# Second half of the causal heads by transfers instead of on-chip transposes, in a pass of a new order, and new order in the early stages

## The chip, the cores and the metric

The kernel runs on 1 core of a Trainium2 chip. The metric is the device time of one execution, in microseconds. A core has TensorE (PE in the profile), VectorE (DVE), ScalarE (ACT), GpSimd (POOL), SyncE (SP, which here issues nearly all DMAs) and 16 DMA engines. Each engine works through its own list of instructions in order; semaphores join them.

## The reference

Per batch (8 of them, 512 tokens x 256 features), all in float32:

```python
h = layernorm(x) * (1 + ca) + sa
x = x + ga * attention(h)          # 16 heads of 16, causal
h = layernorm(x) * (1 + cb) + sb
x = x + gb * ffn_block(h)
# ffn_block: xn = layernorm(h) * ln_g + ln_b
#   o = attention(xn) @ wo + h     # 32 heads of 8, not causal
#   y = gelu(o_half @ w1[e] + b1[e]) @ w2[e] + b2[e]   # two halves of a batch, expert e each
```

sa, ca, ga, sb, cb, gb are rows of silu(c) @ wmod, six per batch. Both attentions take an exact softmax: maximum, exponential, sum, division.

## The kernel before, in words

**Attention steps.** Work goes by *steps* `(b, a, s)`: batch b, a = 0 for the causal attention and 1 for the other, and s counting groups of 4 heads times 4 tiles of 128 queries or keys. A step has 4 slots, one per head. For each head the kernel runs `maxima` (scores by row, TensorE, and their maximum, VectorE), and 8 steps later `scores` (scores by column with the row maximum subtracted inside the matmul, TensorE, then exp on ScalarE), for the causal heads a mask on GpSimd, and `values` (probabilities times v, with a column of ones that gives the sums). Between maxima and scores the row maxima of a group of 4 steps go through DRAM: `max_rows` on GpSimd, `store_max` and, 4 slots later, `load_max` on SyncE, which writes them into q_stack. A group's first scores wait for that load. Full-width maxima take VectorE longer than causal ones, whose width is 128 to 512 keys.

**Normalised heads.** When a group's values are done, ScalarE copies bank_out to out_raw (`sums_out`). Then there are two ways. *By transfers*: out_raw is stored to DRAM (in `sums_out` on SyncE); when both groups of a chunk are there, `load_sums` brings the sums and the heads back with features on the partitions, `invert` (VectorE) takes the reciprocal, `store_inverse` and `load_inverse` spread it over the partitions through DRAM, and `scale_heads` (VectorE, L1806) multiplies. *On the chip*: `normalise` turns out_raw with four transposes (TensorE, L1529), VectorE takes the reciprocals (L1788) and multiplies (L1791), and `head_features` turns the result back with four more transposes (L1539), which ScalarE copies (L1314). `turned_on_chip` says which: before, for the causal heads, batch 0 and the second half (groups 2 and 3) of every batch go on the chip.

**Side work.** Everything else is put beside the steps at fixed slots: `qk` and `v` (projections), `to_features` (transposes of a normalised tile), `attention_out`, `ffn_sum`, `expert_in` with `gelu` (the "cluster"), `expert_out`, `layernorm` in 9 pieces, and the loads and stores. One unit of `qk`, `v`, `attention_out`, `ffn_sum` (a part) or `expert_out` (a part) is 4 matmul instructions. All but the cluster share one PSUM bank, bank_side. The Newton steps of a layernorm's square root run on GpSimd as one piece of 13 small operations, but for batch 0's second and third layernorm on VectorE, which also applies batch 0's modulation (`scale_and_modulate`).

**Stages.** After a prologue, `sections` lays out "before": the causal steps of batches 0, 1 and 2 (48 steps, from 73.5 us), then "run": a first pass of 32 steps of batch 0's second attention, passes n = 1 to 5 of 48 steps, and a tail. A pass has 16 steps of (n, 1), 8 of (n+2, 0), 16 of (n, 1), 8 of (n+2, 0); beside them go batch n+1's output, normalisations and projections, batch n-1's experts, and batch n+3's first normalisation and projections. In `place_pass` a number such as 93 means step 9, slot 3 of the pass. The placements are written out by hand; within half a step an engine meets first the scores, then the maxima, then values and the two hops of the maxima, then the side items.

Of the kernel before, what the change touches and what calls it, by code (L numbers as in the profile page):

```python
# [11 lines left out]
ALU = mybir.AluOpType  # L12
# [30 lines left out]
BATCHES = 8  # L43
SUM_COLUMNS = 64
# [11 lines left out]
NEWTON_PIECE = 3 + GUESS_STEPS  # L56
LN_PIECES = NEWTON_PIECE + 3

# [196 lines left out]
EARLY = 3  # L255
# [37 lines left out]
def place_pass(plan, first, n):  # L293
# [11 lines left out]
    place_units(plan, first, (71, 73), in_pieces("ffn_sum", e, 0))  # L305
    place_units(plan, first, (81, 83), in_pieces("ffn_sum", e, 1))
    place_units(plan, first, (172,), [("keep_x", n)])
    place_units(plan, first, (81, 83), layernorm_items(b, 1)[:2])
    place_cluster(plan, first, 93, e, 0, norm_under(b, 1))
    place_units(plan, first, (103, 111), [("ffn_input", b, 0), ("ffn_input", b, 1)])  # L310
    place_expert_out(plan, first, (101, 103, 113, 123), e, 0, 0)
    place_units(plan, first, (123, 131, 133, 133, 133, 133, 133, 153, 161), layernorm_items(b, 2))
    place_expert_out(plan, first, (133, 143, 153, 163), e, 0, 1)
    place_units(plan, first, (113, 183, 191), [("load_expert_in", e, 1), ("store_y", e, 0), ("load_expert_out", e, 1)])
# [3 lines left out]
    place_units(plan, first, (101, 131), [("load_residual", n + 2), ("load_mod", n + 2)])  # L318
# [19 lines left out]
def place_first_pass(plan):  # L338


    place(plan, 0, [("bias_part", 0, 0), ("load_expert_in", 0, 0), ("load_expert_out", 0, 0)], 0)
# [5 lines left out]
    place(plan, 18, [("load_x", 3)])  # L347
# [5 lines left out]
    place_at(plan, (45, 47), features_items(1, 1))  # L353
# [3 lines left out]
    place(plan, 77, [("stacks", 1, 2)])  # L357
    place_at(plan, (74, 91, 91, 105, 121), heads_items(0, 1, 0))
    place_at(plan, (87, 91, 95, 99), v_items(1, 1))
    place_norm(plan, (80, 82, 84, 85, 85, 85, 86, 94, 96), 3, 0)  # L360
    place(plan, 108, [("stacks", 1, 3)])
    place_at(plan, (101, 103), features_items(3, 0))
    place_at(plan, (105, 107, 109, 111, 115, 119, 123, 127), qk_items(0, 3))
    place(plan, 112, [("load_gate", 1)])
    place(plan, 130, [("keep_v", 1)])
    place_at(plan, (133, 141, 141, 147, 153), heads_items(0, 1, 1))
# [186 lines left out]
def build(nc, x, wq1, wk1, wv1, wo1, ln_g, ln_b, wq2, wk2, wv2, wo2, w1, b1, w2, b2, c, wmod, out):  # L553
# [28 lines left out]
    with ExitStack() as ctx:  # L582
# [193 lines left out]
        def previous_qk(a, b):  # L776


            if a == 0:
                return (1, b - 1) if b >= EARLY else (0, b)  # L780
# [1131 lines left out]
```

## Time and profile before

| | |
|---|---|
| median of 3 runs | 1524.27 us (1523.96 to 1528.13) |
| profiled execution | 1528.74 us, span 1526.7 us |
| TensorE clock granted, mean | 0.983 of full speed |
| DMA, whole run | 204.96 MB, mean 134 GB/s |
| stacks of a causal half batch | 4 DMAs of 256 KB (q) and 4 of 192 KB (k) |
| w_out | 1024 KB, 8.4 us from issue to landing |

The busy shares in 40 slices of the span (each digit is tenths, one slice is 38 us):

```profile
PE   6689798799999999999999999999999989998998
DVE  6577879898687887869687786878778697858621
PEclk9599899999999999999999999999999999999999
```

TensorE is filled less in the first eight slices than later, and its clock is lower in slices 1 and 4. From slice 10 (about 380 us) the picture repeats with each pass.

### The profile page before, as it was taken

The page shows a single profiled execution, that of the slowest core. Times are in us where ns is not written, and L with a number is a line of the kernel's source. Part 1 is how long each engine was busy: PE and PEld are TensorE (multiplying, and loading weights), DVE is VectorE, ACT ScalarE, POOL GpSimd, SP SyncE. Part 2 cuts the span into 40 slices and gives each one's busy share as a digit, 9 for nine tenths or more (in the row PEclk, how much of TensorE's full clock was granted, in tenths as well). Part 3 has the DMA queues.
Part 4 walks back from the last instruction along what each step waited for, and adds up shares of the span by engine and source line. Part 5 has one row for each costly group of instructions (what it writes and reads, how often), then busy time and mean ns, then how long its engine had stood idle before and what let it go on. Part 6 is the DMA issues. An engine that isn't in the chain of part 4 may idle for free.

```text
span 1526.7 us, 29704 instructions
## 1 busy us (share of the span) xinstructions
PE 1403.2 (92%) x9537; PEld 595.7 (39%) x9537; DVE 1143.9 (75%) x2889; ACT 994.3 (65%) x2074; POOL 485.3 (32%) x1217
## 2 busy tenths in 40 slices
PE   6689798799999999999999999999999989998998
PEld 5234242233434334343434334343344323342437
DVE  6577879898687887869687786878778697858621
ACT  1055466677667667776667666676767766767772
POOL 4145243334241334315332243413343133302100
PEclk9599899999999999999999999999999999999999
DMA  6856444347355453835645373654537242525230
GB/s 194 228 124 168 100 142 132 79 144 197 96 171 127 131 149 97 241 84 155 153 135 143 115 194 93 190 136 130 137 107 206 76 127 60 174 76 133 89 124 15
DMA packets 193886, 204.96 MB, mean 134 GB/s; under 512 B 58432, under 2 KB 143744, under 8 KB 193736
## 3 DMA queue, kind: packets, MB, share of 16 engines
q1 hardware_dynamic: 188072, 199.08, 47.8%
q10 hardware_dynamic: 5664, 3.98, 0.9%
q8 instruction: 82, 1.34, 0.4%
q14 instruction: 68, 0.56, 0.1%
HBM read 123.99 MB, written 79.02 MB: 133 GB/s over the span
## 4 chain that ended last, share of the span: by engine, by line
PE 71%; DVE 13%; ACT 7%; issue 3%; DMA 3%; SPq 2%; POOL 1%; DVEq 0%; ACTq 0%; POOLq 0%
PE bank_out L1519 17%; PE bank_scores L1497 13%; PE bank_max L1475 9%; PE bank_side L1436 8%; PE bank_side L1616 6%; DVE max_column L1760 5%; PE bank_max L1596 4%; PE bank_side L1449 3%; ACT probs L1294 3%; PE bank_side L1569 2%; PE bank_side L1596 2%; DVE bank_max L1757 2%; PE bank_side L1557 2%; PE bank_scores L1596 2%; PE bank_side L1411 1%
## 5 line engine op out<-in xcount | busy, mean ns | idle before, releaser
L1294 ACT ACTIVATE probs<-bank_scores 128x512 f32<-128x512 f32 (+3 forms) x1536 | 752.4, 543 | 286.1 <-PE bank_scores L1497 280.2
L1760 DVE TENSOR_REDUCE max_column<-bank_max 128x1 f32<-128x512 f32 x1024 | 653.1, 683 | 106.6 <-PE bank_max L1475 102.0
L1519 PE MATMUL bank_out<-probs,v_tile 128*9 128x512 f32 (+4 forms) x3072 | 364.8, 547 | 4.4 <-issue 1.7
L1475 PE MATMUL bank_max<-k_stack,q_stack 64*128 64x512 bf16 (+3 forms) x2048 | 313.0, 342 | 42.6 <-DVE max_column L1757 14.2
L1497 PE MATMUL bank_scores<-q_stack,k_stack 64*128 64x512 bf16 (+3 forms) x2048 | 315.0, 344 | 35.0 <-ACT probs L1294 34.3
L1757 DVE CUSTOM_DVE_ANT_0 bank_max<-bank_max,causal 128x384 f32<-128x384 f32 (+3 forms) x512 | 241.6, 514 | 103.0 <-PE bank_max L1475 100.9
L1497 PEld LDWEIGHTS bank_scores<-q_stack,k_stack 64*128 64x128 bf16 x2048 | 80.9, 93 | 417.5 <-issue 410.5
L1148 POOL CAST max_parts<-max_row 128x32 bf16<-128x32 f32 x96 | 23.0, 240 | 436.5 <-DVE max_row L1773 436.0
L1475 PEld LDWEIGHTS bank_max<-k_stack,q_stack 64*128 64x128 bf16 x2048 | 104.1, 95 | 116.9 <-issue 78.8
L1616 PE MATMUL bank_side<-w_out,hidden_T 128*128 128x256 f32 x448 | 126.6, 405 | 0.0
L1166 POOL TENSOR_SCALAR_AFFINE_SELECT probs<-probs 128x512 f32<-128x512 f32 x128 | 81.5, 637 | 58.6 <-ACT probs L1294 58.6
L1519 PEld LDWEIGHTS bank_out<-probs,v_tile 128*9 128x9 f32 (+1 forms) x3072 | 47.4, 91 | 129.4 <-issue 97.6
L1616 PEld LDWEIGHTS bank_side<-w_out,hidden_T 128*128 128x128 f32 x448 | 75.9, 189 | 44.6 <-issue 37.3
L1436 PE MATMUL bank_side<-act_T,wq 128*128 128x256 f32 x248 | 72.5, 416 | 8.3 <-DVE act_T L1729 3.7
L1436 PE MATMUL bank_side<-act_T,wk 128*128 128x256 f32 x244 | 70.4, 412 | 2.5 <-DVE rest L1743 1.0
L1757 DVE DVE_READ_ACCUMULATOR2_ANT max_column<- 128x1 f32 x512 | 72.1, 141 | 0.0
L1449 PE MATMUL bank_side<-wv,act_T 128*128 128x256 f32 x244 | 70.2, 411 | 0.5
L1256 ACT ACTIVATE partsq<-bank_side 128x256 bf16<-128x256 f32 x62 | 23.8, 385 | 68.2 <-PE bank_side L1436 68.0
L1134 POOL CAST partsq<-rest 128x256 bf16<-128x256 f32 x64 | 25.4, 396 | 119.0 <-DVE rest L1743 118.9
L1309 ACT ACTIVATE out_raw<-bank_out 128x512 f32<-128x512 f32 x96 | 57.9, 603 | 1.2 <-PE bank_out L1519 1.2
L1436 PEld LDWEIGHTS bank_side<-act_T,wq 128*128 128x128 f32 x248 | 43.8, 196 | 31.4 <-issue 10.5
L1596 PE MATMUL bank_max<-expert_xT,w_in 128*128 128x256 f32 x240 | 54.2, 379 | 0.0
(162 smaller groups left out, 1351.1 us busy)
## 6 DMA issues: line engine op xcount, KB each, us to landing
q_stack<-q_parts SPq DMA_DIRECT2D x124, 256.0 KB, 4.5
k_stack<-k_parts SPq DMA_DIRECT2D x124, 192.0 KB, 6.0
out_raw<-out_raw SPq DMA_DIRECT2D x74, 256.0 KB, 2.1
w_in<-in_L_ffn_w_dram SPq DMA_DIRECT2D x15, 1024.0 KB, 5.1
w_out<-in_L_ffn_w_dram SPq DMA_DIRECT2D x15, 1024.0 KB, 8.4
q_parts<-partsq SPq DMA_DIRECT2D x32, 384.0 KB, 2.7
k_parts<-partsk SPq DMA_DIRECT2D x32, 384.0 KB, 2.8
q_parts<-partsq SPq DMA_DIRECT2D x32, 256.0 KB, 3.1
```

Source lines behind the costliest of these rows:

```text
L1166: pool.affine_select(out=tile, in_=tile, compare_op=ALU.is_ge, fill=0.0, base=0, pattern=[[0, GROUP], [1, P]], channel_multiplier=-1).then ...
L1294: nc.scalar.activation(probs[s % 2][:, head_at(k), q0:S], region[bank][:, q0:S], ACT.Exp, scale=float(WIDTH[a]) ** -0.5).then_inc(drained[ ...
L1309: nc.scalar.activation(out_raw[:, g % 2, :], outb[:, :], ACT.Copy).then_inc(drained["out"], 1)
L1436: ins = pe.matmul(region[bank][:, 0:S // 2], w_qkv[a][t][:, cc, oc * P:(oc + 1) * P], act_T[:, cc, cols], start=(cc == 0), stop=(cc == C - 1))
L1449: ins = pe.matmul(region[bank][:, 0:D], act_T[:, cc, t * P:(t + 1) * P], w_qkv[a][2][:, cc, :], start=(cc == 0), stop=(cc == C - 1))
L1475: ins = pe.matmul(region[to][:, 0:keys], q_stack[buf][rows, at, qt * P:(qt + 1) * P], k_stack[buf][rows, at, 0:keys], start=(i == 0), stop ...
L1497: ins = pe.matmul(region[to][:, q0:S], k_stack[buf][rows, at, kt * P:(kt + 1) * P], q_stack[buf][rows, at, q0:S], start=(i == 0), stop=last)
L1519: ins = pe.matmul(outb[32 * k:32 * k + WIDTH[a] + 1, q0:S], v_tile[a][:, kt, g * GROUP + k, :], probs[s % 2][:, k, q0:S], start=(kt == 0), ...
L1596: ins = pe.matmul(region[bank][:, k * EXP_TOK:(k + 1) * EXP_TOK], w_in_of(b, j)[:, cc, ft * P:(ft + 1) * P], expert_xT[:, cc, j * EXP_TOK: ...
L1616: ins = pe.matmul(region[bank][:, 0:D], hidden_T[:, ft, k * P:(k + 1) * P], w_out_of(b, j)[:, ft, :], start=(ft == 0), stop=(ft == FT - 1))
L1757: v.tensor_tensor_reduce(region[bank][:, 0:keys], region[bank][:, 0:keys], causal[:, S - keys:S], 1.0, -3e38, ALU.add, ALU.max, dst).then_ ...
L1760: v.tensor_reduce(dst, region[bank], AX_X, ALU.max).then_inc(drained[bank], 1)
```

## The change

Four edits. (1) `turned_on_chip`: for batches 3 to 6 the second half of the causal heads goes by transfers; `attention_out` waits for both chunks. (2) `place_pass` in a new order: the transfer chain (b, 0, 1) at steps 2 to 8, `ffn_sum` before `attention_out`, the first cluster at step 12 instead of 9, and all that follows it later; features (b, 1) at steps 43 and 45. (3) Newton steps: never on VectorE; for the layernorms in NEWTON_APART GpSimd runs them in three parts with side slots of their own. Batch 0's modulation goes to GpSimd as for the other batches. (4) The early stages: slots moved; batch 3's first normalisation, features and q/k projections come earlier, its v comes into the first pass.

```diff
-        return b == 0 or g >= HEADS[0] // GROUP // 2
+        return b == 0 or g >= HEADS[0] // GROUP // 2 and not EARLY <= b < BATCHES - 1
+NEWTON_APART = ((2, 0), (0, 1), (0, 2), (3, 0), *((b, 2) for b in range(2, BATCHES - 1)))
...
 def place_pass
-    place_units(plan, first, (3, 13, 61, 63), v_items(0, n + 2))
-    place_units(plan, first, (13,), [("bias_part", n, 0)])
     if n > 1:
-        place_units(plan, first, (23,), [("head_features", b, 0, 1)])
-    place_units(plan, first, (33, 41, 43, 53), out_items(b))
+        place_units(plan, first, (3, 13, 63, 73), v_items(0, n + 2))
+        place_units(plan, first, (13,), [("bias_part", n, 0)])
+        place_units(plan, first, (21, 41, 41, 61, 81), heads_items(b, 0, 1))
+    place_units(plan, first, (83, 93, 103, 113) if n > 1 else (23, 33, 43, 53), out_items(b))
+    place_units(plan, first, (23, 33) if n > 1 else (83, 93), in_pieces("ffn_sum", e, 0))
+    place_units(plan, first, (43, 53) if n > 1 else (103, 113), in_pieces("ffn_sum", e, 1))
-    place_units(plan, first, (71, 73), in_pieces("ffn_sum", e, 0))
-    place_units(plan, first, (81, 83), in_pieces("ffn_sum", e, 1))
-    place_units(plan, first, (81, 83), layernorm_items(b, 1)[:2])
-    place_cluster(plan, first, 93, e, 0, norm_under(b, 1))
-    place_units(plan, first, (123, 131, 133, 133, 133, 133, 133, 153, 161), layernorm_items(b, 2))
+    place_units(plan, first, (111,), layernorm_items(b, 1)[:1])
+    place_cluster(plan, first, 123, e, 0, layernorm_items(b, 1)[1:])
+    place_units(plan, first, (151, 161, 161, 161, 161, 161, 161, 183, 191), layernorm_items(b, 2))
+    place_units(plan, first, (171, 173), [("newton", b, 2, 1), ("newton", b, 2, 2)])
-    place_units(plan, first, (171, 173), features_items(b, 2))
-    place_units(plan, first, (21, 93, 173, 251, 333, 423),
+    place_units(plan, first, (211, 221), features_items(b, 2))
+    place_units(plan, first, (23, 93, 173, 251, 333, 423),
                 [("stacks", n + 2, 0), ("stacks", n, 4), ("stacks", n, 5), ("stacks", n + 2, 1), ("stacks", n + 1, 2), ("stacks", n + 1, 3)])
-    place_units(plan, first, (181, 191, 201, 211, 221, 231, 241, 253), qk_items(1, b))
-    place_units(plan, first, (233, 251), features_items(b, 1))
-    place_units(plan, first, (263, 273, 283, 293), v_items(1, b))
+    place_units(plan, first, (231, 233, 241, 243, 253, 261, 263, 273), qk_items(1, b))
+    place_units(plan, first, (281, 283, 291, 293), v_items(1, b))
+    place_units(plan, first, (433, 453), features_items(b, 1))
...
 def place_first_pass
-    place_at(plan, (51, 53), features_items(1, 2))
-    place_at(plan, (55, 59, 63, 67, 71, 75, 79, 83), qk_items(1, 1))
+    place_at(plan, (59, 63), features_items(1, 2))
+    place_at(plan, (67, 71, 75, 79, 83, 87, 91, 95), qk_items(1, 1))
-    place_norm(plan, (80, 82, 84, 85, 85, 85, 86, 94, 96), 3, 0)
-    place_at(plan, (101, 103), features_items(3, 0))
-    place_at(plan, (105, 107, 109, 111, 115, 119, 123, 127), qk_items(0, 3))
+    place_at(plan, (1, 19, 23, 27, 31, 35, 39, 43), qk_items(0, 3))
+    place_at(plan, (47, 51, 53, 55), v_items(0, 3))
...
 def sections ("before")
-    place_norm(beside, (84, 88, 90, 91, 92, 93, 94, 98, 100), 0, 1)
-    place_norm(beside, (102, 104, 106, 107, 107, 107, 108, 114, 116), 0, 2)
-    place_at(beside, (117, 119), features_items(0, 2))
+    place_norm(beside, (82, 86, 87, 87, 87, 87, 87, 97, 101), 0, 1)
+    place_at(beside, (91, 95), [("newton", 0, 1, 1), ("newton", 0, 1, 2)])
+    place_at(beside, (99, 102, 103, 107), [("ffn_input", 0, t) for t in range(T_STEPS)])
+    place_norm(beside, (105, 110, 111, 111, 111, 111, 111, 121, 123), 0, 2)
+    place_at(beside, (115, 119), [("newton", 0, 2, 1), ("newton", 0, 2, 2)])
+    place_at(beside, (125, 129), features_items(0, 2))
+    place_norm(beside, (138, 142, 143, 143, 143, 143, 143, 155, 159), 3, 0)
+    place_at(beside, (147, 151), [("newton", 3, 0, 1), ("newton", 3, 0, 2)])
+    place_at(beside, (185, 189), features_items(3, 0))
...
 GpSimd
-                if piece == NEWTON_PIECE and not (b == 0 and n):
-                    for step in range(GUESS_STEPS, ROOT_STEPS):
+                if piece == NEWTON_PIECE:
+                    last = GUESS_STEPS + 5 if (b, n) in NEWTON_APART else ROOT_STEPS
+                    for step in range(GUESS_STEPS, last):
                         newton_step(pool, b, n, step)
+            def newton(b, f, n, turn):
+                for step in range(GUESS_STEPS + 1 + 4 * turn, GUESS_STEPS + 5 + 4 * turn):
+                    newton_step(pool, b, n, step)
...
 TensorE, attention_out
-                if (b, 0, 0) in scaled_number:
-                    wait(pe, heads_made, scaled_number[b, 0, 0] + 1)
+                for cc in range(C):
+                    if t == 0 and (b, 0, cc) in scaled_number:
+                        wait(pe, heads_made, scaled_number[b, 0, cc] + 1)
...
 VectorE: scale_and_modulate and the Newton steps of batch 0 are taken out
```

## Rows read from the trace of the kernel before

**Rows 1.** The page: busy time by engine; the chain that ended last.

```profile
PE 1403.2 (92%) x9537; PEld 595.7 (39%) x9537; DVE 1143.9 (75%) x2889; ACT 994.3 (65%) x2074; POOL 485.3 (32%) x1217
...
PE 71%; DVE 13%; ACT 7%; issue 3%; DMA 3%; SPq 2%; POOL 1%; DVEq 0%; ACTq 0%; POOLq 0%
```

**Rows 2.** Stretches: length; busy PE, PEld, DVE, ACT, POOL; clock, DMA share, GB/s.

```profile
140.00:190.00 50.00, 41.37 (x350) 17.81 (x352) 39.39 (x170) 23.66 (x61) 14.74 (x30) 0.90 0.55 120
...
192.00:242.00 50.00, 46.72 (x418) 20.05 (x419) 40.87 (x117) 32.08 (x83) 21.34 (x47) 1.00 0.46 128
...
243.00:286.00 43.00, 33.77 (x230) 10.16 (x230) 38.81 (x86) 28.38 (x55) 21.06 (x56) 1.00 0.47 126
...
292.00:298.00 6.00, 6.00 (x32) 2.04 (x30) 2.58 (x4) 3.78 (x7) 0.00 (x0) 0.72 0.16 49
...
573.68:750.28 176.60, 170.54 (x1181) 71.36 (x1180) 139.33 (x353) 124.33 (x259) 61.48 (x155) 1.00 0.52 143
```

**Rows 3.** TensorE's timeline: start, length, line, operation, count, [idle before].

```profile
266.33 1.05 PE L1519 MATMUL bank_out<-probs,v_tile 128*9 128x512 f32 x8
...
269.11 1.05 PE L1519 MATMUL bank_out<-probs,v_tile 128*9 128x512 f32 x8
...
291.78 0.63 PE L1411 MATMUL bank_side<-ident,normed 128*128 128x128 f32 x4 [3.12 <-DVE normed L1707]
...
345.68 1.13 PE L1436 MATMUL bank_side<-act_T,wk 128*128 128x256 f32 x4 [0.40 <-DVE rest L1743]
...
1325.73 1.05 PE L1519 MATMUL bank_out<-probs,v_tile 128*9 128x512 f32 x8
...
1328.85 1.05 PE L1519 MATMUL bank_out<-probs,v_tile 128*9 128x512 f32 x8
...
1334.79 0.61 PE L1475 MATMUL bank_max<-k_stack,q_stack 64*128 64x512 bf16 x2 [2.17 <-DMA k_stack<-k_parts]
...
1335.33 1.89 PE L1519 MATMUL bank_out<-probs,v_tile 128*9 128x512 f32 x8
```

**Rows 4.** Groups by line in 140 to 190 us, VectorE.

```profile
L886 DVE TENSOR_SCALAR root<-root 128x4 f32<-128x4 f32 x6 | 1.0, 170 | 0.2
...
L1672 DVE SCALAR_TENSOR_TENSOR normed<-normed,rstd,mod_bc 128x256 f32<-128x256 f32 x4 | 2.1, 568 | 0.0
```

**Rows 5.** Groups by line, whole run.

```profile
L1729 DVE TENSOR_SCALAR act_T<-bank_side,mod_cur 128x512 f32<-128x512 f32 x15 | 12.1, 807 | 2.5 <-PE bank_side L1411 2.0
...
L1529 PE MATMUL bank_max<-ident,out_raw 128*128 128x128 f32 x88 | 14.4, 286 | 0.7 <-ACT out_raw L1309 0.7
```

**Rows 6.** TensorE's waits in one pass (573.68 to 750.28): total, times, longest.

```profile
PE bank_side L1436 <- ACT act_T L1281: 0.5, 1, 0.5
...
PE bank_side L1539 <- DVE x_in L1791: 0.4, 1, 0.4
```

**Rows 7.** SyncE's timeline of DMA issues, start of pass 3.

```profile
722.84 2.58 SPq L860 DMA_DIRECT2D q_stack<-q_parts  x4
...
727.52 0.43 SPq L963 DMA_DIRECT2D w_out<-in_L_ffn_w_dram  x1
...
730.85 3.71 SPq L1061 DMA_DIRECT2D max_rows<-max_parts  x3
...
739.30 0.58 SPq L1071 DMA_DIRECT2D q_stack<-max_rows  x2
```

**Rows 8.** A 3 us stretch inside those issues.

```profile
727.00:730.00 3.00, 3.00 (x19) 1.12 (x18) 2.62 (x6) 1.57 (x3) 0.97 (x3) 1.00 1.06 229
```

**Rows 9.** Timeline: a load_max, the scores that waited for it, and step 8's scores.

```profile
102.50 0.57 SPq L1071 DMA_DIRECT2D q_stack<-max_rows  x2
...
104.35 0.61 PE L1497 MATMUL bank_scores<-q_stack,k_stack 64*128 64x512 bf16 x4 [0.17 <-DMA q_stack<-max_rows]
...
743.26 0.39 PE L1497 MATMUL bank_scores<-q_stack,k_stack 64*128 64x512 bf16 x2
```

More of the change, by code:

```diff
@@ L43 @@
 BATCHES = 8
+EARLY = 3
 SUM_COLUMNS = 64
@@ L448, in sections @@
     place_at(beside, (1, 5, 9), qk_items(0, 1)[5:])
-    place_at(beside, (15, 19, 27, 31), v_items(0, 1))
+    place_at(beside, (13, 17, 21, 29), v_items(0, 1))
     place(beside, 3, [("load_x", 2)])
-    place(beside, 12, [("stacks", 1, 0)])
-    place(beside, 43, [("stacks", 1, 1)])
+    place(beside, 18, [("stacks", 1, 0)])
+    place(beside, 39, [("stacks", 1, 1)])
     place(beside, 40, [("load_gate", 0)])
-    place_norm(beside, (14, 18, 22, 24, 24, 25, 26, 32, 34), 2, 0)
-    place_at(beside, (41, 43), features_items(2, 0))
@@ L456, in sections @@
-    place_at(beside, (45, 49, 53, 57, 61, 65, 69, 71), qk_items(0, 2))
+    place_norm(beside, (14, 18, 19, 19, 19, 19, 19, 29, 31), 2, 0)
+    place_at(beside, (23, 27), [("newton", 2, 0, 1), ("newton", 2, 0, 2)])
+    place_at(beside, (33, 37), features_items(2, 0))
+    place_at(beside, (41, 45, 49, 53, 57, 61, 65, 69), qk_items(0, 2))
     place(beside, 67, [("first_v", 1)])
     place_at(beside, (73, 75), [("head_features", 0, 0, 0), ("head_features", 0, 0, 1)])
-    place(beside, 76, [("stacks", 2, 0)])
@@ L460, in sections @@
-    place_at(beside, (77, 79, 81, 83), out_items(0))
-    place_norm(beside, (84, 88, 90, 91, 92, 93, 94, 98, 100), 0, 1)
-    place_at(beside, (85, 89, 93, 97), v_items(0, 2))
-    place_norm(beside, (102, 104, 106, 107, 107, 107, 108, 114, 116), 0, 2)
+    place(beside, 72, [("stacks", 2, 0)])
+    place_at(beside, (77, 79, 81, 85), out_items(0))
+    place_norm(beside, (82, 86, 87, 87, 87, 87, 87, 97, 101), 0, 1)
+    place_at(beside, (91, 95), [("newton", 0, 1, 1), ("newton", 0, 1, 2)])
+    place_at(beside, (99, 102, 103, 107), [("ffn_input", 0, t) for t in range(T_STEPS)])
@@ L464, in sections @@
+    place_at(beside, (89, 97, 105, 113), v_items(0, 2))
+    place_norm(beside, (105, 110, 111, 111, 111, 111, 111, 121, 123), 0, 2)
+    place_at(beside, (115, 119), [("newton", 0, 2, 1), ("newton", 0, 2, 2)])
     place_at(beside, (104, 118, 118, 128, 140), heads_items(1, 0, 0))
-    place(beside, 107, [("stacks", 2, 1)])
+    place(beside, 102, [("stacks", 2, 1)])
     place(beside, 110, [("load_residual", 1)])
-    place_at(beside, (117, 119), features_items(0, 2))
-    place_at(beside, (121, 125, 129, 133, 137, 141, 145, 149), qk_items(1, 0))
+    place_at(beside, (125, 129), features_items(0, 2))
@@ L469, in sections @@
+    place_at(beside, (131, 133, 137, 141, 145, 149, 153, 157), qk_items(1, 0))
     place(beside, 130, [("load_mod", 1)])
     place(beside, 131, [("first_v", 2)])
-    place(beside, 138, [("stacks", 0, 2)])
+    place(beside, 146, [("stacks", 0, 2)])
     place(beside, 143, [("head_features", 1, 0, 1)])
-    place_at(beside, (153, 157, 161, 165), v_items(1, 0))
+    place_at(beside, (161, 165, 169, 173), v_items(1, 0))
     place(beside, 170, [("stacks", 0, 3)])
-    place_at(beside, (169, 173), features_items(0, 1))
+    place_at(beside, (177, 181), features_items(0, 1))
@@ L1169, in ffn_input @@
             def ffn_input(b, f, half):
-                for t in range(2 * half, 2 * half + 2):
-                    wait(pool, normed_made[1], T * (b - 1) + t + 1)
+                tiles = range(half, half + 1) if b == 0 else range(2 * half, 2 * half + 2)
+                for t in tiles:
+                    wait(pool, normed_made[1], T * b + t + 1)
                     pool.tensor_tensor(ffn_x[:, t, :], normed[1][:, t, :], mod_bc[:, 1, :], ALU.mult).then_inc(ffn_scaled, 1)
-                for t in range(2 * half, 2 * half + 2):
+                for t in tiles:
                     wait(pool, ffn_scaled, T * b + t + 1)
@@ L1663, in first_guess @@
                 ins.then_inc(rstd_made[n], 1)
-            def scale_and_modulate(half):
-                for t in range(2 * half, 2 * half + 2):
-                    v.scalar_tensor_tensor(out=ffn_x[:, t, :], in0=x1[:, t, :], scalar=mean_var[:, 1, t, 0:1],
-                                           in1=mod_bc[:, 1, :], op0=ALU.subtract, op1=ALU.mult).then_inc(ffn_scaled, 1)
-                for t in range(2 * half, 2 * half + 2):
-                    wait(dve, ffn_scaled, t + 1)
-                    v.scalar_tensor_tensor(out=ffn_x[:, t, :], in0=ffn_x[:, t, :], scalar=rstd[:, 1, t:t + 1],
-                                           in1=mod_bc[:, 2, :], op0=ALU.mult, op1=ALU.add).then_inc(ffn_x_made, 1)
             def layernorm(b, f, n, piece):
@@ L1694, in layernorm @@
                 elif piece == NEWTON_PIECE:
-                    if b == 0 and n:
-                        for step in range(GUESS_STEPS, ROOT_STEPS):
-                            newton_step(dve, b, n, step)
+                    pass
                 else:
@@ L1702, in layernorm @@
                     dst = normed[n % 2]
-                    if n == 1 and b == 0:
-                        scale_and_modulate(half)
-                        return
                     for t in range(2 * half, 2 * half + 2):
```

36 lines of the change are left out of this document (18 added, 18 removed).

## The prediction

> **What bounds the kernel now.** I read the page first (busy time by engine, chain of waits), then the busy time in chosen stretches, then the waits of TensorE inside one pass, then the timeline of SyncE's transfers. TensorE is busy for 1403.2 of 1526.7 us and carries 71% of the chain [rows 1], but that share is an average of two regimes. In a pass (48 steps; four of them repeat to within 0.02 us) TensorE is busy 170.54 of 176.60 us, VectorE 139.3 and the DMA engines 52% [rows 2]: there, only TensorE's work and its few waits count. In the early stages it is different: in 140 to 190 us TensorE is idle for 8.6 us and its clock is 0.90; in 243 to 286 it is idle for 9.2 us while VectorE is busy for 38.8 of 43 [rows 2]. A step of the non-causal heads takes 3.12 us with one side unit of work (1328.85 less 1325.73) and still 2.78 with none (269.11 less 266.33) [rows 3], since VectorE's maxima fill it. TensorE's own work in a bare step is about 3.12 - 1.06 = 2.06, so a bare step wastes 0.7 us, and where side work stands counts as much as how much there is.
>
> **The early stage (to about 242 us).** (a) Batch 0's two normalisations lose their Newton steps on VectorE: 26 small operations, each 0.17 us with a gap to 0.2, so 5.2 us [rows 4]. (b) scale_and_modulate goes: 8 operations of 0.56 become 4 of about 0.41 (a pass over the same tile), so 2.9 us less. Together VectorE is relieved of 8.1 us, in the stretch 140 to 190 in which TensorE idles 8.6 us and loses a further 5.0 us to the clock (0.10 of 50) [rows 2, 4]. GpSimd takes the Newton steps in three parts and 8 multiplies and adds of a tile; it works 14.7 of 50 us there before [rows 2], so has the time, and its causal masks, queued behind them, have about a step of slack before the values need them. v and output units are also spread one to a step. Bounds: 0 if the masks come late, -13.6 if all is recovered; I take -8.5, near VectorE's relief. (c) Steps 0 to 18 are filled a little more evenly: -1.5 (0 to -3). (d) Batch 3's first normalisation and its two feature transposes come in from the first pass: on VectorE 8 statistics and scalings of 0.41, aggregates and guesses, 4.4 us, and two act_T copies of 0.8 [rows 5]; on TensorE two sets of transposes of 0.6. 192 to 242 has 9.1 us of VectorE free and 3.3 of TensorE [rows 2]. Between +1.2 and +6.0; I take +3. Sum -7.
>
> **The first pass (32 steps, 243 to 360 us).** Its steps 0 and 4 to 10 have no side unit; q and k of batch 3 now stand there, and only steps 30 and 31 stay bare. (d)'s 6.0 us of VectorE are gone, the features of batch 1 no longer wait for a fresh normalisation: that wait was 3.12 us, and the clock behind it 0.72 for 6 us, 1.7 us more [rows 2, 3]. Lost now: 9.2 + 3.1 + 1.7 and some 3 us elsewhere, 17 us. Against this, four v units of 1.06 come in from pass 1 and 1.2 us of transposes leave, +3. If 11 of 17 are recovered: -8 (-3 to -12).
>
> **Pass 1.** Less: four v units 4.2, two sets of normalise transposes 1.2. But steps 0, 1, 6, 7 are now bare: +4 x 0.7 = 2.9. With the edits common to all passes (below, without the transfer chain): -1.5 (-4 to +1). The loads of batch 3's stacks are as tight here, at most +1.
>
> **Passes 2 to 5, each.** Removed: 2 normalise sets and 1 head_features set. A set is four 128x128 transposes; 22 sets took 14.4 us, 0.65 each, 0.6 without the overlap with their neighbours [rows 5]: -1.8. ScalarE's copy of the heads goes; VectorE gets invert and scale_heads for two reciprocals and two products: nothing, as the one has 52 us free in a pass and the other 37. Waits that go with them: x_in 0.4; act_T 0.5, since the features now stand a step ahead of q and k [rows 6]; -0.9, and some 0.5 of smaller ones. Added: q and k now stand in twos within steps 23, 24 and 26. Two such units in a step cost a wait of 0.40 for the bank, as in the row [rows 3]: +1.2. Batch b's second normalisation moves from steps with causal maxima to steps 16 to 19, whose maxima are full width: VectorE has 14.5 us of work there against 12.5 of steps; +0.8 (0 to 2). Two steps hold only features: +0.3. Without the transfer chain's waits each pass gives -0.4 to -0.9; I take -0.9.
>
> Now the transfers. In steps 2 to 5 SyncE issues, in this order: the stacks of batch n+2 at 722.84, w_out at 727.52, store_max at 730.85, load_max at 739.30 [rows 7]. Stacks and w_out are 1.8 and 1.0 MB; the DMA engines are full (share 1.06, 229 GB/s) [rows 8], so store_max takes 3.71 to issue and load_max waits until 739.30. Its rows are usable 1.85 us after its issue starts (102.50 to 104.35), so at 741.15, and step 8's scores, which need them, start at 743.26 [rows 9]: 2.1 us of slack. After the change two side units (6 to 8 were in twos) and two sets of transposes are gone from these eight steps, so step 8 comes 2 x 1.05 + 2 x 0.6 + 0.4 = 3.7 us earlier: 739.6. The transfers are no sooner: the out_raw store, sums and heads loads of batch n+1 are put ahead of the stacks (0.29 MB more in the burst, 1.2 us at that rate, and the load waits for its store to land, 0.7 to 1.7). With nothing added the stall is 1.6; with all of it 4.4. I take 2.9: TensorE waits in every pass for max_rows at step 8. Behind it scale_heads waits for inverse_T, issued after that same load_max; it lands within the stall, so I give it nothing (up to 1). After such a wait the clock may fall: behind the 2.17 us wait at 1334.79 the 1.05 us of values took 1.89 [rows 3], about 2.5 us in all; +1.3 between 0 and 2.5.
>
> The Trainium skill, "DMA: Bandwidth & Descriptors", Queues, rings and completion order, says that each DMA engine consumes its descriptors in ring order. By that rule the 8 KB of max_rows queue behind the 2.8 MB; the trace agrees (issue 730.85, next load 739.30). Were the small stores free to pass, load_max would follow its store at once and the stall would be nil.
>
> So a pass comes to -0.9 + 2.9 + 1.3 = +3.3, four of them +13.2 (-4 to +26). Pass 5 has no batch n+3; the two features (b,1) fall into its bare steps: -0.8. The tail is unchanged.
>
> **Sum:** -7 - 8 - 1.5 + 13.2 - 0.8 = -4.1 us. Against the profiled execution's 1528.74 that is 1524.6; the median of the runs is 4.5 lower, 1524.27, and gives 1520.2.
>
> **Rivals.**
> (A) The chain fits. For it: in all but this one burst of a pass the two hops of the maxima end well before their scores, and 3.7 us of earlier scores against 2.1 of slack is a small difference of large terms; if SyncE reaches the burst earlier by that much, there is no stall and no clock loss: -4.1 - 4 x 4.2 = -20.9, so 1503.4. Against it: the 2.1 us of slack are measured.
> (B) The other side: the full stall. With 4.4 us of wait and 2.5 of clock each pass gives -0.9 + 6.9 = +6.0, four +24: total +6.7, so 1531. Wait and clock together turn the change into a loss from 5.2 us a pass on, as all other terms sum to -20.9 over four passes. For it: both waits of over 2.1 us in the rows are followed by slow matmuls [rows 2, 3]. Against: 4.4 needs every delay of the burst at its upper end.
> (C) The early gain fails: GpSimd's masks or the DMA of the earlier stacks hold the early stage as VectorE did. -4.1 + 12 = +8, 1532. Against: GpSimd is at 30% there.
> (D) The change does not free TensorE: the removed transposes lay beside waits. Then each pass is 1.8 longer: +7, 1527. Against: TensorE is at 97% of a pass.
>
> **How the numbers follow.** Forecast 40% (1513 to 1528), A 27% (1498 to 1513), B 20%, C 8%, D 5%. 0.3% (4.6 us), what this measurement can tell from none, puts the borders at 1519.7 and 1528.8. Faster: A's 27 and nearly half of the forecast, 0.46; same: the rest of it, D and a little of B, 0.28; slower 0.26. The range reaches into A and B: 1502 to 1534.
>
> **What would show it.** Right: 14 normalise sets instead of 22, 26 scale_heads; no Newton steps on VectorE; TensorE idle in 140 to 190 and 243 to 298 halved; in passes 2 to 5, just before the third group's scores, a wait of L1497 on max_rows of 2 to 4 us, four times, some with slow matmuls behind. A period of the passes near 180 us instead of 176.60 confirms the main step; 173 or less confirms A and makes the prediction wrong by 15 us or more; over 182 is B. An early stage that ends no sooner than before is C.

## The result: 25 us slower, and where they are

The changed kernel takes 1549.7 us (median of 4 runs, 1548.1 to 1550.8) against 1524.2 for the kernel before; the ratio is 1.0156, interval 1.0137 to 1.0176. The forecast was 1520.2, range 1502 to 1534. Its profiled execution took 1550.8; its span is 1549.1, 22.4 longer than before (the kernel before was profiled in an execution 4.6 us above its median, so the medians differ by more).

The page of the kernel after, beside [rows 1]: TensorE is busy for as long, with 48 instructions fewer but some of them slow. Of the chain that ended last, TensorE holds seven points less, the DMA two more and SyncE's issues two more.

```profile
PE 1403.3 (91%) x9489; PEld 594.6 (38%) x9489; DVE 1136.8 (73%) x2851; ACT 993.6 (64%) x2070; POOL 494.9 (32%) x1251
...
PE 64%; DVE 14%; ACT 6%; DMA 5%; SPq 4%; issue 4%; POOL 3%; DVEq 0%; POOLq 0%; ACTq 0%
```

Markers split the difference by stage: ScalarE loads gelu's table once at each cluster of expert products, and the second cluster of a pass stands at the same step in both kernels. Timeline of ScalarE after (start, length, line, operation), the second cluster of pass 1 and of pass 5:

```profile
466.40 1.28 ACT L1340 ACT_TABLE_LOAD   x1
...
1202.62 1.28 ACT L1340 ACT_TABLE_LOAD   x1
```

Before, the same two stand at 474.17 and 1180.58. So up to pass 1's marker 7.8 us are gained, in the four periods between the two 29.8 are lost (7.4 each), and behind them another 0.4.

Three of the stretches of [rows 2] in the kernel after (same columns), with one pass as the last:

```profile
140.00:190.00 50.00, 44.10 (x424) 19.38 (x420) 40.83 (x167) 27.71 (x72) 27.57 (x71) 1.00 0.55 120
...
243.00:286.00 43.00, 38.12 (x240) 13.87 (x236) 39.03 (x89) 29.31 (x60) 27.07 (x66) 1.00 0.52 154
292.00:298.00 6.00, 6.00 (x42) 2.36 (x34) 4.75 (x9) 3.82 (x8) 0.00 (x0) 1.00 0.60 194
...
579.67:763.35 183.68, 171.01 (x1169) 70.92 (x1169) 139.46 (x351) 124.19 (x258) 61.48 (x155) 0.98 0.53 143
```

The early stage did what was meant: TensorE is busy for 44.1 of 50 us instead of 41.4, at full clock instead of 0.90, and for 38.1 of 43 instead of 33.8. The slow matmuls of 292 to 298 are gone with the wait before them [rows 3]. The pass is 7.1 longer at a clock of 0.98. TensorE's waits say why. Over the whole run after (total, times, longest):

```profile
PE bank_scores L1513 <- DMA q_stack<-max_rows: 25.3, 5, 5.5
```

TensorE's timeline after, at those five waits (columns as in [rows 3]), with the values behind the third:

```profile
106.00 1.04 PE L1513 MATMUL bank_scores<-q_stack,k_stack 64*128 64x512 bf16 x4 [5.36 <-DMA q_stack<-max_rows]
...
561.28 0.60 PE L1513 MATMUL bank_scores<-q_stack,k_stack 64*128 64x512 bf16 x2 [5.54 <-DMA q_stack<-max_rows]
744.34 0.60 PE L1513 MATMUL bank_scores<-q_stack,k_stack 64*128 64x512 bf16 x2 [4.47 <-DMA q_stack<-max_rows]
...
745.09 1.89 PE L1535 MATMUL bank_out<-probs,v_tile 128*9 128x512 f32 x8
...
928.70 0.60 PE L1513 MATMUL bank_scores<-q_stack,k_stack 64*128 64x512 bf16 x2 [5.16 <-DMA q_stack<-max_rows]
1112.63 0.61 PE L1513 MATMUL bank_scores<-q_stack,k_stack 64*128 64x512 bf16 x2 [4.72 <-DMA q_stack<-max_rows]
```

Four stand at step 8 of passes 2 to 5, as predicted, the fifth in the early stage, where none was. The eight matmuls of values behind the third wait take 1.89 us instead of 1.05. The stretches around the wait at 744 (columns as above) show TensorE idle for 4 us and then at half clock:

```profile
740.00:744.00 4.00, 0.00 (x0) 0.00 (x0) 0.13 (x1) 0.29 (x1) 0.00 (x0) 0.91 0.47 130
744.00:749.00 5.00, 4.53 (x23) 1.75 (x24) 1.97 (x10) 2.53 (x5) 0.91 (x4) 0.50 0.18 55
```

SyncE's issues ahead of that wait, against [rows 7]: the eight stack loads begin behind out_raw, sums and heads of the chain, the store of the maxima takes 7.78 us to issue instead of 3.71, and the store of the inverse stands between it and load_max. Much of the longer issue is an earlier start: the store begins 5.6 us behind the first stack load instead of 8.0, and its issue ends 13.4 us behind that load instead of 11.7.

```profile
717.62 1.68 SPq L1070 DMA_DIRECT2D max_rows<-max_parts  x3
...
721.12 0.62 SPq L1029 DMA_DIRECT2D out_raw<-out_raw  x1
...
723.86 0.63 SPq L1045 DMA_DIRECT2D sums_T<-out_raw  x1
724.53 0.61 SPq L1046 DMA_DIRECT2D heads_T<-out_raw  x1
725.25 2.56 SPq L869 DMA_DIRECT2D q_stack<-q_parts  x4
...
729.92 0.43 SPq L972 DMA_DIRECT2D w_out<-in_L_ffn_w_dram  x1
730.83 7.78 SPq L1070 DMA_DIRECT2D max_rows<-max_parts  x3
738.66 1.43 SPq L1052 DMA_DIRECT2D inverse<-sums_T  x1
...
742.57 0.57 SPq L1080 DMA_DIRECT2D q_stack<-max_rows  x2
```

### The profile page after: what moved, and what is told of

The parts are those of the page before. It is cut to its first block, busy times and chain, and to the rows that moved or that the text cites. A ratio compares the mean times of both kernels' runs of the same rounds, so it can differ in the third digit from the quotient of the medians.

```text
span 1549.1 us, 29604 instructions
## 1 busy us (share of the span) xinstructions
PE 1403.3 (91%) x9489; PEld 594.6 (38%) x9489; DVE 1136.8 (73%) x2851; ACT 993.6 (64%) x2070; POOL 494.9 (32%) x1251
## 4 chain that ended last, share of the span: by engine, by line
PE 64%; DVE 14%; ACT 6%; DMA 5%; SPq 4%; issue 4%; POOL 3%; DVEq 0%; POOLq 0%; ACTq 0%
PE bank_out L1535 15%; PE bank_scores L1513 11%; PE bank_max L1491 8%; DVE max_column L1762 7%; PE bank_side L1452 7%; PE bank_side L1633 6%; PE bank_max L1613 4%; PE bank_side L1465 3%; DMA max_rows<-max_parts 2%; PE bank_side L1574 2%; ACT probs L1310 2%; PE bank_side L1613 2%; PE bank_scores L1613 2%; DVE bank_max L1759 2%; SPq L1070 2%
## 5 line engine op out<-in xcount | busy, mean ns | idle before, releaser
L1465 PEld LDWEIGHTS bank_side<-wv,act_T 128*128 128x128 f32 x244 | 42.4, 193 | 32.5 <-issue 12.4
```

Source lines behind the costliest of these rows:

```text
L1465: ins = pe.matmul(region[bank][:, 0:D], act_T[:, cc, t * P:(t + 1) * P], w_qkv[a][2][:, cc, :], start=(cc == 0), stop=(cc == C - 1))
```

## Experiments

"Period" is the mean length of a pass, measured between the second clusters of pass 1 and pass 5 (the markers above): 176.6 before, 184.1 in the changed kernel. "Hop" is the time from the start of the store of the third group's maxima to the start of the issue of load_max: 11.7 to 12.4 us in the changed kernel's four passes. The expectations were written before each run. Each kernel is the changed one with the edit shown. Ratios are to the kernel before, run beside it.

**1. No chain.** The second half of the causal heads is turned on the chip again; all else stays.

```
-    return b == 0 or g >= HEADS[0] // GROUP // 2 and not EARLY <= b < BATCHES - 1
+    return b == 0 or g >= HEADS[0] // GROUP // 2
-    place_units(plan, first, (21, 41, 41, 61, 81), heads_items(b, 0, 1))
+    place_units(plan, first, (81,), [("head_features", b, 0, 1)])
```

> The changed kernel, but in passes 2 to 5 the second half of the causal heads is turned on the chip as before, with its four transposes at step 8: the order of all the rest stays, so step 8 is due as early as in the changed kernel, and only the chain's transfers (stores of out_raw, loads of sums and heads, the store and load of the inverse) are gone from the burst. Prediction's arithmetic: with nothing added to the burst the wait at step 8 is 1.6 us, with the chain it was put at 2.9 and measured at 4.5 to 5.5; if the chain makes the difference, the wait falls to 1.5 to 2.5, the period to 180 to 182 (the transposes cost 0.6 again), time 1533 to 1542. Rival: the burst of stacks and w_out alone, met by an earlier step 8, makes nearly all of it: wait over 4, period 183.5 or more, time 1547 to 1553. Other rival: no stall at all without the chain, period 177, time 1522.

1534.8 us, ratio 1.0049 (1.0032 to 1.0066), period 179.2. The waits on the maxima over the run (total, times, longest); 5.04 is the early one, so 0.6 are left a pass:

```profile
PE bank_scores L1513 <- DMA q_stack<-max_rows: 7.5, 5, 5.0
```

SyncE's issues in pass 3 of this kernel, and the scores that waited (TensorE):

```profile
714.54 1.65 SPq L1070 DMA_DIRECT2D max_rows<-max_parts  x3
...
720.07 2.60 SPq L869 DMA_DIRECT2D q_stack<-q_parts  x4
...
728.34 3.80 SPq L1070 DMA_DIRECT2D max_rows<-max_parts  x3
...
736.01 0.57 SPq L1080 DMA_DIRECT2D q_stack<-max_rows  x2
...
737.84 0.39 PE L1513 MATMUL bank_scores<-q_stack,k_stack 64*128 64x512 bf16 x2 [0.47 <-DMA q_stack<-max_rows]
```

The chain makes 15 of the 25 us. From the store of the second group's maxima to load_max of the third are 21.5 us here (736.01 less 714.54) and 24.95 with the chain (742.57 less 717.62). Of the 3.5 us between them, 2.1 come because the burst begins later (7.6 us behind that store against 5.5) and 1.4 arise inside it. And step 8 is due 0.6 us later here, since of the three sets of transposes that are back one stands between that store and step 8. 3.5 + 0.6 = 4.1, against the 4.0 by which the waits of this pass differ (4.47 and 0.47).

**2. w_out behind load_max.**

```
-    (402, 513, 453), [("store_y", e, 1), ("load_expert_out", n, 0), ...
+    (402, 533, 453), [("store_y", e, 1), ("load_expert_out", n, 0), ...
```

> The changed kernel with one edit: in passes 1 to 5 the load of w_out (1 MB) is issued two steps later, behind the load of the maxima of the third group instead of ahead of their store. Theory: TensorE's wait of 4.5 to 5.5 us at step 8 is the time that 1.8 MB of stacks and 1 MB of w_out need ahead of 8 KB of maxima; without w_out's 4.4 us (1 MB at 229 GB/s) the wait and the slow matmuls behind it go. Period of the passes 176.5 to 177.5 instead of 184.05, time 1518 to 1524. Rival 1: the stall is made by what the transfer chain adds on SyncE (its stores, loads and their waits), not by bytes: period stays at 183 to 185, time 1546 to 1551. Rival 2: w_out, now issued later, stands before the next hop of the maxima: the wait moves to step 12, period 180 or more, time 1535 or more.

1555.0 us, 1.0187 (1.0165 to 1.0208), period 185.0, so 1.0 us a pass slower still. With only the stacks and the chain ahead, SyncE issues the store in 1.73 us instead of 7.78, and the hop is 8.1 to 8.7 us instead of 11.7 to 12.4:

```profile
732.66 1.73 SPq L1070 DMA_DIRECT2D max_rows<-max_parts  x3
...
740.83 0.57 SPq L1080 DMA_DIRECT2D q_stack<-max_rows  x2
```

The wait on the maxima fell to 1.0 to 2.1 us. But in each pass there is now one of 5.0 to 5.6 us for heads_T, since w_out's 1 MB stands ahead of the chain's inverse_T:

```profile
749.54 2.04 PE L1574 MATMUL bank_side<-wo,heads_T 128*128 128x256 f32 x4 [4.99 <-DVE heads_T L1808]
```

The main theory fell; rival 2 had the mechanism, with another victim. Two things that TensorE waits for stand behind the burst, not one.

**3. w_out at step 10, behind both.** `513` becomes `581 if n + 3 < BATCHES else 513`.

> The changed kernel, but the load of w_out goes behind both the maxima and the inverse of the chain, to step 10, three steps before its first use. When it went to step 5, the wait on the maxima fell from 5.0 to about 1.1 us a pass and a wait of 5.3 for heads_T took its place. Theory: each time the victim is what stands behind w_out's 1 MB in the queues; at step 10 nothing urgent does, so the wait on heads_T goes too and only about 1.1 us on the maxima is left: period 177.5 to 179.5, time 1524 to 1532. Rival: the stacks' 1.8 MB alone hold the inverse as long: heads_T is still waited for by over 2 us, period over 181, time over 1538.

1530.8 us, 1.0035 (1.0017 to 1.0052), period 181.4: between the two. Both waits are there, smaller: 1.25 to 2.1 us for the maxima, 0.85 to 2.0 for heads_T. With the stacks' 1.8 MB and the chain's own transfers ahead, both still come late; no run tells the two apart here.

**4. The chain behind load_max.** The chain's items go from slots (21, 41, 41, 61, 81) to (53, 71, 71, 81, 91), the output units from (83, 93, 103, 113) to (93, 101, 103, 113).

> The changed kernel, but in passes 2 to 5 the transfer chain of the causal heads starts behind the load of the third group's maxima (loads of sums and heads at step 5 instead of 2, store of the inverse at 7, its load at 8, the output units at 9, 10, 10 and 11). Without the chain the wait on the maxima was 0.6 us a pass and the period 179.1; with it ahead of the stacks 5.0 us and 184.05. Theory: it is where the chain's transfers stand, ahead of the stacks and between the store and the load of the maxima, not their 0.29 MB: now the wait is back at about 0.6 and the chain's own saving shows (four transposes sets fewer and the x_in wait: 2.2 us), period 176.5 to 178, time 1520 to 1528. Rival: behind the burst the chain ends too late, TensorE waits for heads_T at step 9 as it did when w_out was put there: period 180 or more, time 1534 or more.

1563.7 us, 1.0248 (1.0225 to 1.027), period 187.6, the slowest, though TensorE waits less for max_rows and heads_T than in experiment 2 (16.9 us in the four passes against 26.2). By the trace the reason is VectorE, which takes its instructions in order: the reciprocals of the sums and the product with the inverse now stand in it while their transfers are under way, and maxima of steps 8 and 9 stand behind them. No run separates this part. VectorE's timeline in this kernel (last: the idle time before and what ended it):

```profile
746.64 0.35 DVE L1801 RECIPROCAL sums_T<-sums_T 128x32 f32<-128x32 f32 x1 [2.72 <-DMA sums_T<-out_raw]
...
755.81 0.69 DVE L1808 TENSOR_TENSOR heads_T<-heads_T,inverse_T 128x512 f32<-128x512 f32 x1 [3.61 <-DMA inverse_T<-inverse]
```

The clock meanwhile, in a stretch of the same kernel:

```profile
749.00:757.00 8.00, 4.90 (x27) 1.40 (x26) 2.67 (x12) 3.64 (x7) 0.70 (x3) 0.50 0.41 119
```

Neither theory had this: the wait on the maxima did fall, to 0.4 to 2.6 us, and the rival named the wait for heads_T (2.4 to 3.9 us), but neither named what stands behind it on VectorE.

**5. The burst in ScalarE's queue.** SyncE leaves out stacks (n+2, 0) and w_out in passes 2 to 5, ScalarE issues them at the same slots.

```
+            def stacks_too(b, f, u):
+                if not by_scalar("stacks", b, u):
+                    return stacks(b, f, u)
+                ...
+                load_stack(act, b, u, q_dram, q_stack, TILE_ROWS)
+                load_stack(act, b, u, k_dram, k_stack, products)
```

> The changed kernel, but in passes 2 to 5 the burst of step 2 and 3, the stacks of batch n+2 (eight transfers, 1.8 MB) and w_out (1 MB), is issued by ScalarE at the same slots instead of by SyncE. The bytes and their time stay; only the queue is another. Theory: the maxima and the chain's inverse wait because they stand behind the burst in the same queue, not because the DMA engines are full: now they pass, the waits on max_rows (5.0 us a pass) and the slow matmuls behind them go, no wait on heads_T takes their place. ScalarE's exponentials come later by its nine issues (4.6 us at SyncE's 0.5 us each), which may cost TensorE up to that: period 176.5 to 181, time 1520 to 1537. Rival: it is the engines' bandwidth; the maxima share it with the burst and are still waited for by 3 us or more: period 182 or more, time over 1541.

1546.3 us, 1.0131 (1.0103 to 1.016), period 182.8. In the passes no wait of 1 us on max_rows or heads_T is left, as the theory said; its time is missed, since ScalarE issues for 5.1 us and its exponentials stand behind. Nor does this run show that the maxima pass the burst: TensorE's delay puts their store 12 to 13 us behind the first stack load instead of 5.2 to 5.6. ScalarE's timeline in this kernel (ACTq is its DMA issue):

```profile
725.11 2.39 ACTq L869 DMA_DIRECT2D q_stack<-q_parts  x3
727.53 2.10 ACTq L869 DMA_DIRECT2D k_stack<-k_parts  x4
729.73 1.77 ACT L1319 ACTIVATE probs<-bank_scores 128x512 f32<-128x512 f32 x3 [4.35 <-issue]
```

And TensorE, which waits for those exponentials:

```profile
730.48 0.43 PE L1538 MATMUL bank_scores<-q_stack,k_stack 64*128 64x512 bf16 x2 [3.42 <-ACT probs L1319]
```

**6. The same, spread.** The eight loads at slots (23, 31, 33, 41, 43, 51, 53, 61), w_out at step 7, so behind the maxima.

> As the kernel whose burst ScalarE issues, but the eight loads of the stacks stand one to a half step (steps 2 to 6) instead of in a row, and w_out follows at step 7. When they stood in a row the waits on max_rows and on heads_T were gone, but ScalarE's sequencer issued for 5.1 us while the exponentials waited, and TensorE waited 3.4 to 5.3 us for probs, with the clock at half behind it. Theory: with 0.6 us at a time in ScalarE's gaps neither wait is left; what remains is the change's pass without any stall, 179.1 less 0.6 (the last wait on the maxima) less 2.2 (four transposes sets and the x_in wait), plus up to 2 for the eight delays: period 176 to 179, time 1517 to 1529. Rival: the exponentials have no slack, each issue delays TensorE by its 0.6 us: period 181 or more, time 1537 or more. Other rival: the last parts land too late for the maxima at step 8: a wait on q_stack or k_stack there.

1525.0 us, 1.0005 (0.9987 to 1.0022), period 178.2, both in the expected range. SyncE's hop of the maxima in this kernel:

```profile
724.63 1.70 SPq L1083 DMA_DIRECT2D max_rows<-max_parts  x3
...
729.65 0.58 SPq L1093 DMA_DIRECT2D q_stack<-max_rows  x2
```

Two stretches of it, around that hop:

```profile
721.00:725.00 4.00, 4.00 (x27) 1.03 (x30) 3.87 (x9) 2.98 (x7) 0.91 (x4) 1.00 1.00 233
725.00:729.00 4.00, 4.00 (x28) 0.74 (x20) 3.77 (x7) 3.00 (x6) 0.00 (x0) 1.00 0.83 198
```

With the DMA engines nearly as full (share 1.00 and 0.83) the hop takes 5.0 us (5.0 to 6.3 in the four passes) instead of 11.7. Three things differ from the changed kernel: w_out is no longer ahead, the stacks are in another queue, and they are spread. Experiment 2 has the first alone: there SyncE already issues the store in 1.73 us and the hop is 8.3 on average. So of the 6.3 us by which the hops differ on average (12.1 and 5.8), 3.7 go with w_out's place and 2.5 with the other queue and the spreading together; no run separates those two. Three passes still wait 1.1, 1.7 and 2.5 us for heads_T, which the theory did not expect. One has neither wait and shows what the change is without its stall:

```profile
573.49:749.98 176.49, 168.43 (x1169) 70.12 (x1169) 139.33 (x351) 124.25 (x259) 61.84 (x155) 1.00 0.53 149
```

TensorE's waits in that pass (total, times, longest):

```profile
PE bank_scores L1543 <- ACT probs L1323: 3.3, 4, 1.4
...
PE bank_max L1521 <- DVE max_column L1792: 2.0, 5, 0.7
...
PE bank_side L1482 <- DVE rest L1775: 0.8, 2, 0.4
```

TensorE has 2.1 us less to do than in [rows 2] (168.43 against 170.54), and the pass is only 0.1 shorter. The new order takes it back in small waits: before, the same pass had 2.3 on probs, 0.6 on the maxima and none on rest. The changed kernel's own pass has the same three sums (3.3, 2.0, 0.8), so the spread issues on ScalarE add nothing to them.

**7. The early part alone.** The passes of the kernel before behind the new early stage and first pass.

> The changed kernel's early stage and first pass with the passes of the kernel before (causal heads turned on the chip, first cluster at step 9, no Newton step apart, inverses of the first pass's second half at the slots of before); pass 1 keeps out v and bias_part, which the first pass has done. Theory: the early part of the change is worth what stands at pass 1's second cluster, 7.8 us, and the passes cost the other 30: time 1515 to 1518. Rival: the gain read there is lent by the new order of pass 1, which holds less work until that point: time 1520 to 1524.

1520.1 us, 0.9966 (0.9952 to 0.9981). The second cluster of pass 1 is 6.0 us earlier than before and every pass takes 176.6. The time is 2 us over the theory's range and in the rival's: 1.8 of the 7.8 us were lent by the new order of pass 1, which holds less work up to that marker.

**8. Its two stalls mended.** Stacks (1, 0) from slot 18 to 12, stacks (1, 2) from 85 to 81.

> As the kernel with the early part alone, and with two edits: the stacks of batch 1's first unit back at slot 12, those of its third unit at slot 81 instead of 85. With the whole change these gave 3.3 to 4 us up to pass 1. Theory: 1511 to 1514, which beats both kernels. Rival: what is gained early is lost to VectorE's maxima at the border of the first pass: 1516 or more.

1516.1 us, 0.9936 (0.9919 to 0.9952): faster than both kernels by 0.6% and 2.2%. It is 2 us above the expected range, at the lower edge of the rival's, since the first wait shrinks to 2.5 us and doesn't go; the second goes. The stacks stand where they did before, but step 8 is due 2.5 us sooner.

**9. Those stacks behind load_max** (slot 23 instead of 12).

> The kernel with the early part alone and mended, with one difference: the stacks of batch 1's first unit go behind the load of the maxima for step 8 (slot 23) instead of ahead of their store (slot 12), where TensorE still waited 2.5 us for them with slow matmuls behind. Theory: nothing large is ahead of those maxima any more, the wait goes, the stacks are loaded by step 12 in time: 2.5 to 4 us, time 1512 to 1514. Rival: the stacks are now late for the maxima of batch 1, or the next group's maxima queue behind them: 1516 or more.

1520.4 us, 0.9966 (0.9952 to 0.9979). No better than experiment 7: the wait on the maxima is gone, but the stacks come too late for the next batch:

```profile
108.00 0.39 PE L1490 MATMUL bank_max<-k_stack,q_stack 64*128 64x128 bf16 x4 [6.82 <-DMA k_stack<-k_parts]
```

**10. Newton steps on VectorE.** Experiment 8's kernel, batch 0's 26 steps back on VectorE.

```
+                    if b == 0 and n:
+                        for step in range(GUESS_STEPS, ROOT_STEPS):
+                            newton_step(dve, b, n, step)
```

> The mended early-part kernel (1516.1) with one edit undone: batch 0's 26 Newton steps go back to VectorE. Theory: they are 5.2 us of VectorE's time in the stretch in which its maxima hold TensorE, so they come back almost whole: 3 to 6 us, time 1519 to 1522. Rival: the units spread one to a step made the gain, VectorE has room for the steps again: 1515 to 1517.

1524.2 us, 0.9995 (0.9982 to 1.0009): 8.1 us more than with them on GpSimd, more than the theory's 3 to 6. The marker of pass 1 is 8.5 us later. The first row is 140 to 190 us of experiment 8, the second of this kernel:

```profile
140.00:190.00 50.00, 44.06 (x417) 19.11 (x416) 39.64 (x162) 29.26 (x74) 27.61 (x71) 1.00 0.55 111
```

```profile
140.00:190.00 50.00, 39.26 (x348) 15.94 (x340) 39.89 (x169) 22.63 (x60) 19.44 (x37) 0.93 0.55 112
```

TensorE is busy for 4.8 us less there, and at 0.93 of the clock.

**11. Stacks (1, 0) at slot 12 in the whole change.**

> The changed kernel with one edit in the early stage: the stacks of batch 1's first unit are issued at slot 12 as before, not at slot 18, so ahead of the store of the next maxima by more. Theory: the wait of 5.36 us on max_rows at 106 us and the low clock behind it (0.50 to 0.74 for 8 us) are again stacks ahead of the maxima in the queues; both go: 5.4 plus 2 us, time 1541 to 1544. Rival: the stacks only push another transfer there (the k parts that the stacks read are stored no sooner), the wait stays over 3: time 1546 to 1550.

1545.7 us, 1.0125 (1.0104 to 1.0145): 4 us less, not 6 to 8, since 3.45 of the 5.36 us wait stay.

**12. The edits of experiments 2 and 8 together, on the whole change.**

> The changed kernel with the edits of both (w_out behind the third group's load, stacks of batch 1's first unit at slot 12) and a third: the stacks of batch 1's third unit one step earlier (slot 81 instead of 85), against the k_stack wait of 2.11 us at 326 us and the slow step behind it. Theory: -29.8 (four passes back to 176.6), -7.4, -2.1 to -4.5: time 1507 to 1513, faster than the kernel before by 11 to 17 us. Rival: the gains don't add up, because the early stage's gain turns into waits on VectorE: 1515 to 1524.

1547.8 us, 1.014 (1.012 to 1.016), far from the expected 1507 to 1513. It carries experiment 2's loss: 19.4 us in four waits for heads_T. The early edits gain 7 us on experiment 2.

## Why the prediction was wrong, by its own steps

The time is 29.5 us above the forecast. The four passes make 16.6 of it (29.8 lost instead of 13.2), the part up to pass 1's second cluster 8.7 (7.8 gained instead of 16.5), what lies behind pass 5's marker 1.2 (0.4 lost instead of 0.8 gained), and 3.1 come from comparing medians instead of the profiled spans.

- **Passes, the stall, 2.9 (1.6 to 4.4): the step that failed.** Its place, its cause and its four occurrences were right. Measured are 4.5 to 5.5 us, mean 5.0, above the upper bound. Step 8 is due 3.7 us earlier, exactly as worked out: 22.2 us behind the store of the second group's maxima instead of 25.9. What was mis-sized is the chain. The "1.6 with nothing added" was nearly right: experiment 1 has 0.6 on average with step 8 due 0.6 later, so about 1.2. But the chain was given 1.3 of delay (2.9 less 1.6), 2.8 at most (4.4 less 1.6), and it makes 3.5 in pass 3 (experiment 1) and 3.8 on average (5.0 less 1.2). Its bytes were priced right (1.2, measured 1.4 inside the burst). The start of the burst was not: it comes 2.1 us later, for which the prediction counted the wait of the chain's load for its store (0.7 to 1.7) but not SyncE's issues ahead of the burst, 0.62 + 0.63 + 0.61 us.
- **Passes, the clock, 1.3 (0 to 2.5):** mis-sized with it. 7.4 a pass less 5.0 and less -0.1 leaves 2.5, the upper bound, and behind each of the five waits of 4.5 us or more a stretch of 5 to 6 us has a granted clock of 0.50 to 0.52. That is rival B's mechanism with both prices at or over its ends: B gave +6.0 a pass, measured +7.4, and by the prediction's own sign a period over 182 is B.
- **Early stage, term (a), VectorE's relief, -8.5:** the mechanism was right, the size of the whole term is open. The Newton steps alone (5.2 of VectorE's 8.1 us) cost 8.1 when undone; no run undoes the modulation. By operations they are under 6 us. The clock, which the prediction had in its 5.0 us [rows 2], fell again with them, to 0.93, and is the likely rest; no run separates it.
- **What it lacked there:** the stalls of moved stacks. It gave the early DMAs no term and named them only in rival C ("the DMA of the earlier stacks"), at 8%. The load of stacks (1, 0), moved from slot 12 to 18, stands ahead of the load of step 8's maxima. That load is issued at 98.28, but its scores start at 106.00, 7.7 us later, where it was 1.85 before [rows 9]:

```profile
96.22 2.02 SPq L869 DMA_DIRECT2D k_stack<-k_parts  x4
98.28 0.61 SPq L1080 DMA_DIRECT2D q_stack<-max_rows  x2
```

How far the changed kernel is ahead of the kernel before shows in the first exponential of each step on ScalarE: 2.7 us ahead at step 7 (98.03 against 100.68), 2.1 behind at step 8 (107.12 against 105.05). A second wait, for k_stack at 328.80, takes 2.11 us, and from step 72 (326.79 against 330.84) to 73 (333.69 against 334.01) another 3.7 are lost. Together 8.4, near the 8.7 that are missing up to pass 1's second cluster. Undoing shows part of it: experiment 8 is 4.0 us faster than 7 (5.35 at the marker of pass 1) with 2.5 us of the first wait left. Experiment 8 starts the first pass 6.8 us and pass 1 12.2 us ahead of the kernel before, against 7 and 15 predicted; the changed kernel is 3.1 and 5.4 ahead there. So rival C's sign, an early stage that ends no sooner, did not come, though its cause was at work.
- **Passes, the edits, -0.9:** the removed work was right, the waits were not. Transposes 1.8, measured 2.1 less work; q and k in twos 1.2, measured 0.8 (rest); the second normalisation 0.8, measured 1.4 (max_column, at steps 17 to 20). Not foreseen were 1.0 on probs: behind the first cluster at its new place TensorE waits 1.41 us, before 0.25. Sum -0.1 (experiment 6).
- **Rival A (27%)** is refuted: in no kernel with chain and burst both in SyncE's queue did all passes go without a wait on the maxima or on heads_T.
- **scale_heads "within the stall, so nothing":** right only as long as the stall stands. The moves that shortened the wait on the maxima brought it out: waits of 5.0 to 5.6, of up to 2.0, and with VectorE's part a period of 187.6. None of the single moves tried mended the change.
- **Rival D** (no work saved) is refuted by 168.43 us of TensorE's work against 170.54. **Tail and pass 5:** +0.4 together, where -0.8 was predicted.

How much of the store's 7.78 us depends on the bytes ahead of it can be said in part. Its issue ends 11.1 to 12.3 us behind the first stack load where the chain isn't ahead of the burst (before, experiments 1 and 4) and 13.0 to 13.6 where it is (the changed kernel, experiment 11). The 1.3 us that 0.29 MB need at 229 GB/s (an estimate from [rows 8]) would be about that difference. Not settled is the share of the number of transfers against that of their bytes; no run changed the one without the other.

## What to carry to other kernels

In every kernel here, a small transfer that TensorE waited for came late when large ones stood ahead of it in SyncE's queue. So for every such transfer behind a burst count the bytes ahead, and also the issue times and the waits that delay the start of the burst; then ask which transfer is waited for next once the first is served. The stalls of 4.5 us and more cost half as much again through the slow matmuls behind them. And an order that saves 2 us of TensorE's work in a pass can pay it back in waits of 0.4 to 1.4 us.

## What was not expected of the hardware

- The issue of three small stores took 1.7 us with a short queue, 1.73 behind stacks and chain (experiment 2), 3.71 behind stacks and w_out [rows 7], and 7.78 where it began 2.4 us sooner behind these and the chain's 0.29 MB stood ahead too. It is SyncE's time, so all behind it on SyncE was late as well. The Trainium skill, "DMA: Bandwidth & Descriptors", Queues, rings and completion order, has the descriptors of one queue on a DMA engine consumed in order. The trace agrees: at 98.28 the load of the maxima was issued with the stacks just ahead of it and could be used only 7.7 us later. That the bytes in another queue delay it less fits experiment 6 (a hop of 5.0 us at a DMA share of 1.00 and 0.83), but there they were also fewer and spread.
- Issued by ScalarE in a row, the same eight transfers cost TensorE 3.4 to 5.3 us of waiting for exponentials in each pass; with 0.3 to 0.6 us of issuing in each half step they cost none that the waits show.
- The clock fell to 0.50 for 5 us behind the wait of 4.47 (744 to 749 us). In experiment 6 the four matmuls behind a wait of 1.66 us took 1.10 us; behind one of 2.51 the same four took 2.05 (its TensorE timeline):

```profile
913.69 1.10 PE L1604 MATMUL bank_side<-wo,heads_T 128*128 128x256 f32 x4 [1.66 <-DVE heads_T L1838]
...
1092.69 2.05 PE L1604 MATMUL bank_side<-wo,heads_T 128*128 128x256 f32 x4 [2.51 <-DVE heads_T L1838]
```
